# A two-layer graph kernel: the second scatter of the edges' sums is split 73 to 25 between two layers in place of 49 to 49

## The chip, the cores and the metric

The kernel runs on one core of a Trainium2 chip. A core has a matrix engine (TensorE, "PE" in the profile, with its weight loads as "PEld"), a vector engine (VectorE, "DVE"), a scalar engine (ScalarE, "ACT"), GpSimd ("POOL") and a sync engine ("SP") that here only issues transfers. 16 DMA engines carry out all transfers. The metric is the device time of one execution in microseconds (us), lower is better. A profiled execution gives a trace beside its time.

## The reference

A graph network over 50,000 nodes with 256 features each and 12,500 edges, sorted by destination. Only what touches the stages below is shown:

```python
edge_feat = gelu((x[src] + edge_attr) @ W_pre + b_pre) * bases     # 12500 x 256
aggr = segment_sum(edge_feat, dst, num_segments=50000)
y = x + aggr
h = relu(bn(y @ W1 + b1, g1, be1))        # bn: mean and variance over all 50,000 nodes
h = relu(bn(h @ W2 + b2, g2, be2))
x = layernorm(x + (y + h))                # = layernorm(2*x + aggr + h)
# then a second, relational layer on 10,000-odd rows reached by edges, and a last layernorm
```

The first layernorm needs 2x + aggr + h. The kernel keeps one array `y` in device memory. First it holds x + aggr, which the two layers read. For the last step it has to hold x + aggr/2, because the third stage multiplies it by two. So aggr is scattered into `y` twice: first whole, and later once more with the factor -1/2.

## The kernel before, in words

One program per engine; the order of the work is written out by hand and engines wait for each other by semaphores. The nodes are cut into 98 blocks of 512 rows, the edges into 98 tiles of 128 edges. The stages, with their times in the profiled execution:

- **Edges** (to about 255 us): messages per edge, their sums per destination in the array `sums` in on-chip memory; x is copied to `y`.
- **Layer 1** (blocks g = 0 to 97, about 230 to 622 us): SyncE loads block g of `y` into a ring of four buffers (line 713), PE turns it (eight transposes, line 767), ACT and DVE split it into two parts (lines 795 and 848), PE multiplies each block in 24 wide matmuls over three precisions (lines 58 to 60), DVE takes the batch statistics of the product (line 564, two instructions per block), ACT copies the product out of PSUM into one of four `d_h` buffers (`out`, line 817) and SyncE stores it to `scratch_h` (line 719). ACT's copy of a block waits until the store of four blocks earlier has landed. The last four blocks stay on chip (`d_held`) and are not stored.
- **Between the layers**: DVE joins the statistics (lines 594 to 606). One step of it is done by POOL, `coef_pool` (line 610, a power of -1/2). Nothing of layer 2 can start before it.
- **Layer 2** (g = 98 to 195, about 626 to 953 us): the same products with other weights. A block comes from `scratch_h`, passes ReLU with the batch-norm coefficients (line 803), and its product goes to `scratch_h` again.
- **Third stage** (`dense3`, to about 1385 us) and the relational layer (`edges1`, to the end).

POOL carries out both scatters. A tile of 128 sums is one indirect DMA with addition into rows of `y` (`scatter_tile`, line 616). The first scatter runs from 206 us into layer 1. Then comes the second one, `take_back(t)` for t = 0 to 97. Each call waits on three things: that ACT has multiplied the tile's piece of `sums` by -1/2 (`halve`, line 822), that PE has turned every block of `y` into which the tile's rows fall (`passed`), and that the scatter four tiles earlier has landed. Between two of them POOL has to run `coef_pool`. A number, `early`, says how many of the 98 tiles stand ahead of it. POOL runs its instructions in order, so all tiles ahead of `coef_pool` are issued first. The third stage may not read `y` before all 98 have landed.

Of the kernel before, what the change touches and what calls it, by code (L numbers as in the profile page):

```python
# [644 lines left out]
def dense12(nc, A, K, S, c, used, block, first):  # L645
# [9 lines left out]
        return used[-1]  # L655

    NB, ET = S.NB, S.ET
    early = ET // 2
    passes = [(1, k) for k in range(NB)] + [(2, (NB - HELD + n) % NB) for n in range(NB)]
    loads = [g for g, (layer, k) in enumerate(passes) if layer == 1 or k < NB - HELD]  # L660
    stores = [g for g, (layer, k) in enumerate(passes) if layer == 2 or k < NB - HELD]
# [962 lines left out]
def build(nc, A, nodes, edges):  # L1624
# [9 lines left out]
    with ExitStack() as c:  # L1634
# [11 lines left out]
        with ExitStack() as inner:  # L1646
# [33 lines left out]
            block = inner.enter_context(nc.Block())  # L1680
            first = edges0(nc, A, K, S, inner, used, block)
            second = dense12(nc, A, K, S, inner, used, block, first)
            dense3(nc, A, K, S, inner, used, block, second)
        edges1(nc, A, K, S)
# [64 lines left out]
```

How the kernel before makes its waits and increments, by code:

```python
def wait(engine, semaphore, value):  # L72
    if not (isinstance(value, int) and value <= 0):
        engine.wait_ge(semaphore, value)
# [114 lines left out]
    @block.sync  # L190
# [1 line left out]
        def load_attr(k):  # L192
            if k >= 4:
                sp.wait_ge(lo_done, k - 3)
            sp.dma_start(attr[:, k % 4], A["attr_t"][k]).then_inc(attr_full[k % 4], 16)
# [1 line left out]
        def load_bases(k):  # L197
            if k >= 3:
                sp.wait_ge(msg_done, k - 2)
            sp.dma_start(bases[:, k % 3], A["bases_t"][k]).then_inc(bases_full[k % 3], 16)
        sp.dma_start(K.src[:], A["src_t"]).then_inc(src_full, 16)
        sp.dma_start(run_i[:], A["dst_r"]).then_inc(run_full, 16)
        sp.dma_start(before_i[:], A["before_r"]).then_inc(run_full, 16)
        load_attr(0)
        sp.dma_start(raw_w0, A["w0"]).then_inc(w0_full, 16)
        sp.dma_start(K.cols[:], A["cols"]).then_inc(cols_full, 16)
        load_attr(1)
        load_bases(0)
        sp.wait_ge(run_done, 1)
        sp.dma_start(A["cont"].rearrange("(t p) -> t p", p=P), run[:]).then_inc(run_kept, 16)
        sp.dma_start(dst_i[:], A["dst_t"]).then_inc(index_full, 16)
        sp.dma_start(nxt_i[:], A["next_t"]).then_inc(index_full, 16)
# [1 line left out]
        sp.dma_start(last_i[:], A["tile_last"]).then_inc(index_full, 16)  # L215
        sp.dma_start(rel_i[:], A["rel_r"]).then_inc(rel_i_full, 16)
        sp.wait_ge(run_kept, 16)
        sp.dma_start(cont[:], A["cont"].rearrange("(a e) -> a e", a=1).to_broadcast([P, S.TC * P])).then_inc(cont_full, 16)
```

## Time and profile before

| | |
|---|---|
| median of 3 runs | 2051.4 us (2044.15 to 2055.25) |
| profiled execution, its own time | 2051.5 us |
| its span | 2049.7 us |
| granted TensorE clock, mean over the span | 0.957 |
| layer 1: last block's statistics | 621.7 us |
| layer 2: first and last block's statistics | 635.3 and 952.0 us |
| second scatter: tiles 0 to 48, last issued at | 561.2 us |
| second scatter: tiles 49 to 97, issued | 626.3 to 728.2 us |

The page of the profile gives the busy share of each engine over the whole span, but the kernel is a sequence of stages with different limits. So the numbers of use here are those of a stretch: how often a block comes out, what the engines wait for in that stretch, and how long a transfer takes from its issue to its landing. A block's statistics (line 564) are a good clock: two instructions per block, and those that read `pU` and those that read `pS` belong to alternate blocks.

### The profile page before, as it was taken

The numbers are of one execution on the slowest core, as the hardware profiler recorded it, in microseconds if no ns is written. First come the engines' busy times: TensorE is split into PE (matmuls) and PEld (weight loads), VectorE is DVE, ScalarE is ACT, GpSimd is POOL, SyncE is SP. The second block draws the span as 40 slices with busy tenths as digits, with TensorE's granted clock in tenths as the row PEclk, the third lists the DMA queues.
The fourth block names the chain that finished last, engine by engine and source line by source line (L and its number), as shares of the span: only waits on it lengthen the run. The fifth ranks groups of instructions, "written<-read, shape, count | busy, mean of one in ns | idle before, by whom it ended". The sixth has DMA issues, their size and how long they took to land. (4 is left out here: it accounts for less than half of the span.)

```text
span 2049.7 us, 27458 instructions
## 1 busy us (share of the span) xinstructions
PE 1797.7 (88%) x8697; PEld 1401.3 (68%) x8697; DVE 1604.4 (78%) x2326; ACT 1298.1 (63%) x1818; POOL 1074.7 (52%) x1200
## 2 busy tenths in 40 slices
PE   4577589999998889998999999955999999999994
PEld 3465468888886566675666666634887888888883
DVE  4688456767667889996999999984787888888883
ACT  2334346666656788886788888862665666666663
POOL 7456546767706820000555656557787764444443
PEclk9899799999999999999999999987999999999997
DMA  9999999999997999998999999965555422222210
GB/s 351 360 356 396 356 358 337 337 343 330 339 303 199 340 360 325 337 321 318 351 386 386 388 388 383 392 254 161 160 159 170 124 80 69 69 71 74 65 42 28
DMA packets 194033, 541.42 MB, mean 264 GB/s; under 512 B 27013, under 2 KB 77295, under 8 KB 193506
## 3 DMA queue, kind: packets, MB, share of 16 engines
q1 hardware_dynamic: 136354, 414.86, 55.4%
q0 software_dynamic: 47136, 73.62, 15.6%
q10 hardware_dynamic: 10400, 51.20, 6.5%
q8 instruction: 70, 1.15, 0.2%
q14 instruction: 73, 0.60, 0.1%
HBM read 341.49 MB, written 253.66 MB: 290 GB/s over the span
## 5 line engine op out<-in xcount | busy, mean ns | idle before, releaser
L616 POOL DMA_INDIRECT scratch_y<-sums,k_target x196 | 315.2, 1608 | 159.8 <-issue 72.4
L1005 ACT ACTIVATE d_o<-d_u,d_free 128x256 f32<-128x256 f32 x392 | 203.2, 589 | 66.3 <-POOL d_free L1042 66.3
L978 PE MATMUL d_pN<-d_y,d_free 128*128 128x512 f32 x392 | 193.3, 616 | 43.0 <-DVE d_u L1068 34.0
L983 PEld LDWEIGHTS d_pN<-k_ident,d_r 128*128 128x128 f32 x1568 | 191.5, 193 | 47.3 <-issue 46.8
L58 PE MATMUL pU<-d_part_h,k_w_h 128*128 128x512 f32 x392 | 166.3, 424 | 38.5 <-DVE d_part_l L860 17.1
L983 PE MATMUL d_pN<-k_ident,d_r 128*128 128x128 f32 x1568 | 191.6, 276 | 0.0
L848 DVE TENSOR_TENSOR d_part_l<-pT,d_part_h 128x1024 fp32r<-128x1024 f32 x98 | 119.9, 1224 | 86.0 <-ACT d_part_h L795 86.0
L795 ACT ACTIVATE d_part_h<-pT 128x1024 fp32r<-128x1024 f32 x98 | 100.5, 1026 | 132.1 <-PE pT L767 118.4
L58 PE MATMUL pS<-d_part_h,k_w_h 128*128 128x512 f32 x392 | 165.5, 422 | 15.3 <-ACT d_h L817 9.2
L1039 POOL TENSOR_TENSOR d_free<-d_free,k_minus_half 128x8 f32<-128x8 f32 (+1 forms) x100 | 163.7, 1637 | 0.2
L1068 DVE SCALAR_TENSOR_TENSOR d_u<-d_pN,d_free,k_base 128x256 f32<-128x256 f32 x392 | 161.1, 474 | 0.0
L254 POOL DMA_INDIRECT k_ring<-in_x,k_src x100 | 121.9, 1219 | 68.3 <-PE pT L282 39.8
L994 ACT ACTIVATE d_r<-d_h,k_coef 128x512 f32<-128x512 f32 x196 | 147.7, 800 | 15.5 <-DMA d_h<-scratch_h 15.5
L59 PE MATMUL pU<-d_part_l,k_w_h 128*128 128x512 f32 x392 | 156.6, 400 | 0.0
L60 PE MATMUL pU<-d_part_h,k_w_l 128*128 128x512 f32 x392 | 156.3, 399 | 0.0
L60 PE MATMUL pS<-d_part_h,k_w_l 128*128 128x512 f32 x392 | 156.0, 398 | 0.0
L59 PE MATMUL pS<-d_part_l,k_w_h 128*128 128x512 f32 x392 | 155.8, 398 | 0.0
L610 POOL TENSOR_TENSOR d_bn_rstd<-d_bn_var,k_minus_half 128x2 f32<-128x2 f32 x2 | 1.5, 730 | 281.1 <-DVE d_bn_var L597 281.1
L1433 ACT ACTIVATE e_gate<-pG,k_gate_b 128x512 f32<-128x512 f32 (+1 forms) x150 | 98.3, 672 | 76.8 <-PE pG L60 76.7
L803 ACT ACTIVATE d_r<-k_ring,d_coef 128x512 f32<-128x512 f32 x188 | 141.7, 803 | 0.0
L978 PEld LDWEIGHTS d_pN<-d_y,d_free 128*128 128x128 f32 x392 | 67.1, 191 | 106.0 <-issue 105.4
L1241 POOL DMA_INDIRECT e_xd<-out,k_dst_gather x98 | 124.6, 1272 | 26.7 <-issue 26.7
(219 smaller groups left out, 4946.3 us busy)
## 6 DMA issues: line engine op xcount, KB each, us to landing
scratch_h<-d_h SPq DMA_DIRECT2D x192, 512.0 KB, 7.7
out<-d_o SPq DMA_DIRECT2D x97, 520.0 KB, 5.9
k_ring<-scratch_y SPq DMA_DIRECT2D x98, 512.0 KB, 7.7
d_h<-scratch_h SPq DMA_DIRECT2D x98, 512.0 KB, 7.0
d_y<-scratch_y SPq DMA_DIRECT2D x98, 512.0 KB, 7.8
scratch_y<-in_x ACTq DMA_DIRECT2D x25, 2000.0 KB, 19.7
k_ring<-scratch_h SPq DMA_DIRECT2D x94, 512.0 KB, 5.6
attr<-in_attr_t SPq DMA_DIRECT2D x25, 512.0 KB, 15.2
```

The source lines that it names most:

```text
L58: pe.matmul(out, lhs[0], rhs[0], start=first, stop=False)
L59: pe.matmul(out, lhs[0], rhs[1], start=False, stop=False)
L60: return pe.matmul(out, lhs[1], rhs[0], start=False, stop=last)
L616: pool.indirect_dma_start(out=A["y"], out_offset=bass.IndirectOffsetOnAxis(ap=K.target[:, t:t + 1], axis=0), in_=K.sums[:, t], in_offset=N ...
L803: last = act.activation(r[:, g % 2, cc], source(g)[:, cc * B:(cc + 1) * B], ACT.Relu, bias=coef[:, 1, cc:cc + 1], scale=coef[:, 0, cc:cc + 1])
L978: pe.matmul(pN[k % 4][:, 2 * two:2 * two + 2].rearrange("p j f -> p (j f)"), twice[:], y[:, k % 4, two * 2 * F:(two + 1) * 2 * F], start=T ...
L983: last = pe.matmul(pN[k % 4][:, j, cc * P:(cc + 1) * P], r[:, k % 4, cc, j * P:(j + 1) * P], K.ident[:], start=False, stop=j % 2 == 1 and ...
L994: last = act.activation(r[:, k % 4, cc], h2[:, k % 4, cc * B:(cc + 1) * B], ACT.Relu, bias=K.coef2[:, 1, cc:cc + 1], scale=K.coef2[:, 0, c ...
L1005: last = act.activation(o[:, k % 4, j, 0:F], u[:, k % 3, j], ACT.Identity, bias=nb[:, n, j:j + 1], scale=rs[:, n, J + j:J + j + 1])
L1039: pool.tensor_tensor(out=rs[:, at, now], in0=v[:, at, now], in1=K.minus_half[:, now], op=ALU.pow).then_inc(rs_done, 1)
L1068: last = dve.scalar_tensor_tensor(out=u[:, k % 3, j], in0=pN[k % 4][:, j], scalar=rs[:, (k - 3) % 4, j:j + 1], in1=K.base[:], op0=ALU.mult ...
L1241: pool.indirect_dma_start(out=xd[:, k % 2, j], out_offset=None, in_=A["out"], in_offset=bass.IndirectOffsetOnAxis(ap=K.dst_gather[:, t:t + ...
```

## The change

One number: of the 98 tiles, three quarters (3 * 98 // 4 = 73) are scattered ahead of `coef_pool` instead of half (49). 24 tiles move from behind the layers' boundary to the end of layer 1.

```diff
     NB, ET = S.NB, S.ET
-    early = ET // 2
+    early = 3 * ET // 4
...
         for t in range(early):
             take_back(t)
         coef_pool(pool)
         for t in range(early, ET):
             take_back(t)
```

Only POOL's program moves; the rows on the other engines stay as they are. First place: POOL behind tile 48, before. L616 is the scatter of a tile, L736 the reading of its `passed` value, L610 the power of `coef_pool`.

```order
L736 TENSOR_LOAD k_passed
L736 ISA x2
L616 DMA scratch_y<-sums,k_target 50000x256
L610 TENSOR_TENSOR d_bn_rstd<-d_bn_var,k_minus_half 128x2
L736 TENSOR_LOAD k_passed
```

The same place of the changed kernel:

```order
L736 TENSOR_LOAD k_passed
L736 ISA x2
L616 DMA scratch_y<-sums,k_target 50000x256
L736 TENSOR_LOAD k_passed
L736 ISA x2
L616 DMA scratch_y<-sums,k_target 50000x256
```

The power no longer follows tile 48; the tiles go on. Second place: POOL behind tile 72 of the changed kernel, 24 tiles later.

```order
L736 TENSOR_LOAD k_passed
L736 ISA x2
L616 DMA scratch_y<-sums,k_target 50000x256
L610 TENSOR_TENSOR d_bn_rstd<-d_bn_var,k_minus_half 128x2
L736 TENSOR_LOAD k_passed
L736 ISA x2
```

Here the power stands now, with 25 tiles behind it instead of 49.

## Rows read from the trace of the kernel before

**Rows 1.** The page: the whole span, and PE and DMA in 40 slices.

```profile
span 2049.7 us, 27458 instructions
PE 1797.7 (88%) x8697; PEld 1401.3 (68%) x8697; DVE 1604.4 (78%) x2326; ACT 1298.1 (63%) x1818; POOL 1074.7 (52%) x1200
...
PE   4577589999998889998999999955999999999994
...
DMA  9999999999997999998999999965555422222210
```

**Rows 2.** Windows of both layers: busy us of each engine (instructions), clock, DMA share, GB/s.

```profile
440.00:550.00 110.00, 110.00 (x600) 92.32 (x599) 76.78 (x99) 68.00 (x70) 76.60 (x51) 1.00 1.09 336
550.00:574.00 24.00, 23.60 (x124) 18.99 (x123) 16.01 (x19) 14.05 (x14) 10.20 (x7) 1.00 1.07 346
574.00:620.00 46.00, 46.00 (x250) 38.58 (x249) 31.67 (x39) 23.32 (x24) 0.00 (x0) 1.00 0.93 288
620.00:635.00 15.00, 6.72 (x20) 5.00 (x19) 7.24 (x14) 7.45 (x9) 8.22 (x6) 0.66 0.27 30
680.00:740.00 60.00, 49.18 (x195) 35.31 (x196) 46.59 (x60) 46.20 (x57) 40.96 (x26) 1.00 1.09 346
740.00:950.00 210.00, 200.49 (x796) 144.16 (x795) 194.66 (x253) 180.29 (x219) 0.00 (x0) 1.00 0.96 328
```

**Rows 3.** Line 564, every second block, six stretches: duration, first and last start.

```profile
L564 DVE BATCH_NORM_STATS2 stats<-pU x68: 680/690/702, 301.3 to 544.4; 128x6 f32<-128x512 f32 x68
...
L564 DVE BATCH_NORM_STATS2 stats<-pU x7: 682/699/700, 551.3 to 574.8; 128x6 f32<-128x512 f32 x7
...
L564 DVE BATCH_NORM_STATS2 stats<-pU x14: 680/692/700, 574.8 to 619.5; 128x6 f32<-128x512 f32 x14
...
L564 DVE BATCH_NORM_STATS2 d_stats<-pU x16: 681/687/699, 635.3 to 680.4; 128x6 f32<-128x512 f32 x16
...
L564 DVE BATCH_NORM_STATS2 d_stats<-pU x18: 680/687/700, 679.8 to 739.9; 128x6 f32<-128x512 f32 x18
...
L564 DVE BATCH_NORM_STATS2 d_stats<-pU x30: 680/688/700, 771.9 to 860.1; 128x6 f32<-128x512 f32 x30
```

**Rows 4.** POOL's scatters (line 616) in three stretches, the same columns.

```profile
L616 POOL DMA_INDIRECT scratch_y<-sums,k_target x7: 1541/1541/1542, 549.4 to 561.2; - x7
...
L616 POOL DMA_INDIRECT scratch_y<-sums,k_target x26: 1535/1636/2513, 626.3 to 680.4; - x26
...
L616 POOL DMA_INDIRECT scratch_y<-sums,k_target x23: 1541/1543/2294, 682.2 to 728.2; - x23
```

**Rows 5.** ACT's waits in 550 to 574, then in 680 to 740: total us, times, longest.

```profile
ACT d_h L817 <- DMA scratch_h<-d_h: 8.8, 6, 1.9
...
ACT d_h L817 <- DMA scratch_h<-d_h: 14.6, 14, 1.5
```

**Rows 6.** Stores, median us to landing: 540-560, 580-600, 640-660, 700-720.

```profile
scratch_h<-d_h SPq DMA_DIRECT2D x5, 512.0 KB, 12.5
...
scratch_h<-d_h SPq DMA_DIRECT2D x6, 512.0 KB, 5.1
...
scratch_h<-d_h SPq DMA_DIRECT2D x6, 512.0 KB, 9.0
...
scratch_h<-d_h SPq DMA_DIRECT2D x6, 512.0 KB, 12.3
```

**Rows 7.** What the added tiles wait for: ACT's halving (all), PE's transposes up to 562 us.

```profile
L822 ACT ACTIVATE sums<-sums x25: 1046/1062/1062, 292.8 to 559.8; 128x1024 f32<-128x1024 f32 x25
...
L767 PE MATMUL pT<-k_ident,k_ring x664: 270/273/418, 230.9 to 559.8; 128*128 128x128 f32 x166
```

**Rows 8.** POOL in order of time: start us, us, [idle before <- what ended it].

```profile
625.01 0.73 POOL L610 TENSOR_TENSOR d_bn_rstd<-d_bn_var,k_minus_half 128x2 f32<-128x2 f32 x1 [62.24 <-DVE d_bn_var L597]
...
736.22 0.56 POOL L1019 TENSOR_SCALAR d_free<-k_ident 128x128 f32<-128x128 f32 x1 [6.00 <-DMA scratch_y<-sums,k_target]
```

**Rows 9.** DMA queues in 440 to 560 us: packets, MB, share of 16 engines.

```profile
q1 hardware_dynamic: 9301, 33.87, 74.1%
q0 software_dynamic: 7890, 6.37, 34.3%
...
scratch_y<-sums,k_target POOLq DMA_INDIRECT x56, 7.8
```

## Prediction, made before the changed kernel was run

> **What bounds the kernel now.** I began with the page [rows 1]. PE is busy 88% of the span, DMA stands at 9 tenths from the start to slice 25 or so, and neither says what a moved scatter is worth, since the layers at issue cover only 230 to 953 us. So I read windows inside the layers [rows 2]. At 440 to 550 us PE is busy for all 110 us while DMA's share is already at 1.09: PE sets the pace, DMA is full beside it. At 680 to 740 us, with scatters running in layer 2, PE is busy only 49 of 60 us and DMA again at 1.09: there DMA sets the pace. Once the scatters are over (740 to 950) PE is at 200 of 210 and DMA at 0.96.
>
> The third view is the clock of blocks [rows 3]. The rows hold two instructions for every second block, and "last" is the second of its pair, 0.6 us after the first. This gives us per block:
> - layer 1 with scatters, 301.3 to 543.8: 66 blocks, 3.67.
> - 551.3 to 574.8: 6 blocks, 3.92.
> - layer 1 without scatters, 574.8 to 618.9: 12 blocks, 3.67.
> - layer 2 with scatters, first part, 635.3 to 679.8: 14 blocks, 3.18.
> - second part, 679.8 to 739.3: 16 blocks, 3.72.
> - layer 2 without scatters, 771.9 to 859.4 or so: 28 blocks, 3.125.
>
> So the scatters cost nothing for a long time and then something. The waits name the place [rows 5]: in both slow stretches ACT's copy of the product (line 817) waits for the store of four blocks earlier. The landing times say why it comes late [rows 6]: a store lands in 5.1 us without scatters, 9.0 us shortly after they begin in layer 2, 12.3 and 12.5 us in the slow stretches. DMA falls behind a little with each block, the backlog grows for about 50 us of layer 2 until four buffers no longer cover it, and only then do blocks slow down. That is the idea on which everything below rests.
>
> **The change part by part.** 24 tiles (49 to 72) are issued from 563 us on instead of behind `coef_pool`. Nothing is added or removed; each costs POOL the same and moves the same bytes.
>
> *Can they be issued there?* Three waits. Halving: the last of 25 pieces is multiplied at 559.8 us [rows 7], so all are ready. The transposes: destinations are sorted and spread evenly, so tile t of 98 needs about t + 2 blocks turned; tile 72 needs about 74. By 562 us 664 transposes of 8 per block are done, 83 blocks [rows 7]. The third wait is the scatter four tiles back, and sets the rate: 7 scatters from 549.4 to 561.2, 1.97 us each [rows 4]. So 24 more end at 561.2 + 24 x 1.97 = 608.5 us. POOL is wanted again for the power at 625.0 and idles 62.24 us before it [rows 8]; 16 us of that would be left. `coef_pool` is not late. It would be, if a scatter took over 2.66 us (63.8/24), as none in a group of rows does on average: 26 of them take 54.1 us in layer 2, 2.16 each.
>
> *Layer 1's end.* The stretch 574.8 to 618.9 now runs beside scatters, with DMA's backlog already at its limit: ACT waits for stores in 550 to 574. The steady price there is the pace after the backlog has bitten: about 4.0 us a block (3.92 on average over 6 blocks, of which the first and last are at the turn), 0.33 over the 3.67 of PE. The blocks that can be hit are those between 563 and the last scatter's end, about 12. Three of them are slow already in the kernel before, since the backlog takes that long to go (blocks until 574.8). That leaves 9 blocks x 0.33 = 3.0 us lost. The bounds: 0, if the slow blocks at 550 to 574 were a passing thing, since for the 66 blocks before them scatters at the same rate cost nothing; and 12 x 0.6 = 7 us, if blocks here slow by as much as those of layer 2 did (3.72 - 3.12). I take 3.0, from the nearest rows.
>
> *The boundary.* The last stores of layer 1 are those of the blocks before the held four. DMA's share between 620 and 635 us is 0.27 [rows 2], and the last moved tile should have landed by about 617 (608.5 + 7.8, the median to landing [rows 9]). The backlog has time to empty, so layer 2 starts as it does now. Price 0.
>
> *Layer 2.* What the scatters cost here before: 14 blocks x (3.18 - 3.125) = 0.8 us, 16 blocks x (3.72 - 3.125) = 9.5 us, together 10.3. Now 25 tiles stand behind the power instead of 49. The first 26 of before are issued from 626.3 to 680.4 [rows 4], so the last of the 25 goes out at about 678.5. This is where the expensive part begins. The 0.8 us stays. The backlog that has built up has to go: in both places of before the slow pace outlasts the last scatter by about three blocks, which at 0.5 each is 1.5 us. So 2.3 us stay and 8.0 go. The bounds: 9.5 gone (no tail), and half of 10.3, 5.1 (if the price per scatter were even). I take 8.0. What is late next when the store wait goes is PE's own pace at 3.125.
>
> *Behind layer 2.* The third stage may read `y` from 953 on; the scatters were through at 736 [rows 8] and will be through near 687. Nothing waits for them either way: 0. From there on everything moves forward by what the two layers gained.
>
> The sum: 2051.5 (the profiled execution's own time, which is the 2049.7 of the span and 1.8 around it) + 3.0 - 8.0 = 2046.5 us. The median of the runs shown is 2051.4, so I take the sum for the median too. A difference under 0.5%, 10.3 us, can't be told from no change by a measurement of this kernel, whose three runs are 11.1 us apart. The forecast is 0.24% down.
>
> *A page weighed against the rows.* Between 440 and 560 us the 56 scatters occupy 34.3% of the 16 engines and the rest 74.1% [rows 9], together over 100: the two kinds of traffic do compete. The Trainium skill (DMA: Bandwidth & Descriptors, "Issuing engines are not separate DMA queues") says that transfers issued by sync, scalar and GpSimd end up on the same 16 DMA engines and interleave. By this rule alone the change would be worth nothing, because the same work waits in the same queue at another time; that is rival B. The trace agrees that the engines are shared, and shows that the price is not even: 66 blocks of layer 1 paid nothing.
>
> **The rivals.**
> - *A: layer 1 takes the tiles free.* For it: 3.67 us a block over 66 blocks with scatters; 550 to 574 may be the crest of a wave. Against it: the landing time had climbed to 12.5 us when the slow blocks came, and scatters that go on leave it no reason to fall. Time: 2051.5 - 8.0 = 2043.5; with no tail in layer 2 as well, 2042.
> - *B: the price moves with the tile.* 24 of 49 tiles take half of 10.3 = 5.1 us with them and cost the same in layer 1. For it: DMA is at 1.07 to 1.09 in both places. Against it: PE needs 3.67 us a block in layer 1 and 3.125 in layer 2, so layer 1 leaves DMA 0.55 us a block more. Time: 2051.5.
> - *C, the slower side: the backlog is carried over the boundary.* If the moved tiles' traffic is not through when layer 2's first stores and loads go out, at about 637 us, layer 2 starts with buffers already late and pays from its first block: 14 blocks x 0.6 = 8.3 us and the tail of 1.5, so 9.8 of the 10.3 stay, while layer 1 has lost 3 to 7. Time: 2051.5 - 0.5 + 3 to 7 = 2054 to 2058. It decides only if scatters take over 2.66 us each; then `coef_pool` is late too. Against it: DMA's 0.27 in 620 to 635 and the 16 us left on POOL.
> - *D: the tiles do not move in time*, because tile 49 to 72 wait for their blocks. By [rows 7] nothing of it is to be seen: they go out at once. It would be 2051.5 with a late power.
>
> **How the numbers follow.** Forecast 0.55, A 0.20, B 0.14, C 0.09, D 0.02. The forecast's own bounds are 3.0 lost (0 to 7) and 8.0 gained (5.1 to 9.5): 2042 to 2053.4. The median of a few runs adds some us either way. A range of 2040 to 2054.5 holds the forecast, A, B and the lower end of C. Faster by over 0.5% means below 2041.1: A with runs that fall low, and a small part of the forecast, 0.13. Slower by over 0.5%, above 2061.7: C beyond what I worked out, 0.04. Within 0.5%: 0.83.
>
> **What would show it.** In the changed kernel's profile:
> - POOL: 24 more scatters from 563 to about 609 us, then some 16 us idle before line 610, which starts near 628.
> - Line 564 at 575 to 611 us: 4.0 us a block instead of 3.67; ACT's line 817 waits for `scratch_h` stores there, which land in 12 us.
> - Layer 1's last statistics at about 624.7 instead of 621.7.
> - Layer 2: blocks at 3.18 for the first 14, two or three slow ones, then 3.125; the store wait of 14.6 us [rows 5] shrinks to 2 or so.
> - Layer 2 ends about 5 us earlier than 952.
>
> I am wrong if the blocks at 575 to 611 stay at 3.67 (A), if line 610 starts after 632 or the first blocks of layer 2 already wait for stores (C), or if layer 2 shows 3.4 us a block for all the time that scatters run (B).

## The result, and the profile after

The changed kernel takes 2042.87 us (median of 16 runs), the kernel before 2048.82 us (16 runs). The ratio is 0.9963, with a 95% interval of 0.995 to 0.9976: 5 to 10 us faster. The forecast was 5.0 us faster. The profiled executions are further apart, 2049.7 against 2042.5 us of span, and only part of those 7.2 us belongs to the change. The single times of one kernel spread over more than the difference (2042.12 to 2057.48 and 2036.13 to 2046.78 us), so what the change did is read from the stages of the traces.

POOL first: the moved tiles in layer 1 (with the tile before them), then the tiles of layer 2 (line 616 of the kernel after; count, min/median/max ns, first and last start, as in [rows 4]):

```profile
L616 POOL DMA_INDIRECT scratch_y<-sums,k_target x25: 1541/1541/1543, 561.0 to 610.1; - x25
...
L616 POOL DMA_INDIRECT scratch_y<-sums,k_target x25: 1535/1632/2441, 627.7 to 679.8; - x25
```

The 24 moved tiles went out from 563 to 610.1 us, 2.05 us apart (24 intervals in the 49.1 us from 561.0), and 25 were left for layer 2. POOL at the boundary, as in [rows 8]:

```profile
626.43 0.73 POOL L610 TENSOR_TENSOR d_bn_rstd<-d_bn_var,k_minus_half 128x2 f32<-128x2 f32 x1 [14.74 <-DVE d_bn_var L597]
```

POOL still waits 14.74 us for DVE before the power of `coef_pool`. So nothing at the boundary is late because of the moved tiles. The scatters are through at about 688 instead of 736 us.

Windows of the kernel after, for three of the stretches of [rows 2]:

```profile
574.00:620.00 46.00, 45.73 (x244) 37.52 (x243) 30.43 (x37) 25.43 (x25) 28.34 (x19) 1.00 1.09 343
620.00:635.00 15.00, 6.73 (x23) 5.01 (x22) 8.35 (x15) 7.45 (x9) 7.12 (x5) 0.71 0.35 82
680.00:740.00 60.00, 55.54 (x222) 39.85 (x221) 52.98 (x68) 50.84 (x62) 3.26 (x2) 1.00 1.01 346
```

Two lines changed most. At 574 to 620 DMA is now at 1.09 instead of 0.93, yet PE still gets through 45.73 of 46 us. At 680 to 740 PE is busy 55.5 us instead of 49.2. ACT's waits for stores in 574 to 620 and in 680 to 740 (before: none and 14.6 [rows 5]):

```profile
ACT d_h L817 <- DMA scratch_h<-d_h: 15.2, 11, 1.7
...
ACT d_h L817 <- DMA scratch_h<-d_h: 4.0, 3, 1.5
```

The 15.2 us of waiting in 574 to 620 cost the blocks only about 1.5 us; why is said at the end of the experiments. For the length of layer 2 I take line 564 over the whole of it. The first block reads `pU`, the last reads `pS`, so the length runs from the first start of the one row to the last start of the other. Before, then after:

```profile
L564 DVE BATCH_NORM_STATS2 d_stats<-pU x98: 680/687/700, 635.3 to 949.6; 128x6 f32<-128x512 f32 x98
L564 DVE BATCH_NORM_STATS2 d_stats<-pS x98: 497/682/700, 638.6 to 952.6; 128x6 f32<-128x512 f32 x96, 128x6 f32<-128x336 f32 x2
```

```profile
L564 DVE BATCH_NORM_STATS2 d_stats<-pU x98: 680/686/700, 636.9 to 944.4; 128x6 f32<-128x512 f32 x98
L564 DVE BATCH_NORM_STATS2 d_stats<-pS x98: 496/682/700, 640.0 to 947.4; 128x6 f32<-128x512 f32 x96, 128x6 f32<-128x336 f32 x2
```

That is 952.6 - 635.3 = 317.3 us before and 310.5 us after: layer 2 is 6.8 us shorter. The end of layer 2 comes 5.2 us earlier (947.4 against 952.6), because layer 1 had begun 1.6 us later in this execution. The other 2.0 us of the span's 7.2 arise in the relational layer, behind everything that was changed.

### The profile page after: what moved, and what is told of

Same layout as the page of the kernel before. It is cut to its first block and busy times, and to the rows that moved or that the text cites. A ratio compares the mean times of both kernels' runs of the same rounds, so it can differ in the third digit from the quotient of the medians.

```text
span 2042.5 us, 27458 instructions
## 1 busy us (share of the span) xinstructions
PE 1795.9 (88%) x8697; PEld 1398.3 (68%) x8697; DVE 1604.1 (79%) x2326; ACT 1297.4 (64%) x1818; POOL 1067.5 (52%) x1200
## 3 DMA queue, kind: packets, MB, share of 16 engines
q1 hardware_dynamic: 136354, 414.86, 55.5%
## 5 line engine op out<-in xcount | busy, mean ns | idle before, releaser
L616 POOL DMA_INDIRECT scratch_y<-sums,k_target x196 | 312.0, 1592 | 159.7 <-issue 71.4
L610 POOL TENSOR_TENSOR d_bn_rstd<-d_bn_var,k_minus_half 128x2 f32<-128x2 f32 x2 | 1.5, 729 | 275.9 <-DVE d_bn_var L597 275.9
```

The source lines that it names most:

```text
L616: pool.indirect_dma_start(out=A["y"], out_offset=bass.IndirectOffsetOnAxis(ap=K.target[:, t:t + 1], axis=0), in_=K.sums[:, t], in_offset=N ...
```

## The experiments

All differ from the kernel before by the lines shown (e5 from the changed kernel). "Paced" means that POOL holds each tile back until a certain number of blocks is done. Two lengths are read from each trace, both from the starts of the statistics: layer 2 as above, and the last 40 block intervals of layer 1, less the 146.05 us that they take when nothing waits for a store (146.06 in six of the traces). This difference is the price in layer 1. The ratio isn't the quotient of the two medians, and differs from it by up to 0.0024.

| kernel | tiles in layers 1 / 2 | layer 1 price, us | layer 2, us | median | before, run beside it | ratio (95%) |
|---|---|---|---|---|---|---|
| before | 49 / 49 | 1.6 | 317.3 | 2048.82 | | |
| after | 73 / 25 | 1.5 | 310.5 | 2042.87 | 2048.82 | 0.9963 (0.9950 to 0.9976) |
| e1 | 49 / none | 0.0 | 306.6 | 2039.76 | 2052.61 | 0.9952 (0.9934 to 0.9970) |
| e2 | 49 / 25 | 0.0 | 310.7 | 2044.66 | 2052.61 | 0.9965 (0.9948 to 0.9982) |
| e3 | 24 / 74 | 0.0 | 323.6 | 2057.77 | 2052.61 | 1.0035 (1.0020 to 1.0050) |
| e4 | 80 / 18 | 0.0 | 307.5 | 2046.78 | 2052.61 | 0.9974 (0.9958 to 0.9990) |
| e5 | 73 / 25 paced | 2.6 | 308.1 | 2044.36 | 2053.11 | 0.9945 (0.9923 to 0.9967) |
| e6 | 49 / 49 paced | 0.0 | 307.1 | 2042.71 | 2053.11 | 0.9946 (0.9932 to 0.9959) |
| e7 | 49 / 49, 3 buffers | 3.5 | 327.2 | 2068.08 | 2053.11 | 1.0064 (1.0047 to 1.0081) |
| e8 | 98 / none | 1.7 | 306.5 | 2078.96 | 2053.11 | 1.0125 (1.0108 to 1.0143) |
| e9 | 49 / 49 | 1.4 | 318.7 | 2084.57 | 2085.13 | 0.9997 (0.9969 to 1.0024) |
| e10 | 73 / 25 | 1.5 | 310.1 | 2084.57 | 2085.13 | 0.9988 (0.9953 to 1.0023) |
| e11 | 44 / 54, both paced | 0.0 | 309.5 | 2074.38 | 2085.13 | 0.9972 (0.9943 to 1.0002) |
| e12 | 49 / 49 paced | 0.6 | 307.2 | 2074.85 | 2085.13 | 0.9954 (0.9918 to 0.9990) |

### e1: no tiles in layer 2

```diff
-        for t in range(early, ET):
+        for t in range(early, LEFT):        # LEFT = 49, and the waits at the end for as many
             take_back(t)
```

> Left out of the computation: tiles 49 to 97 of the second scatter, all those of layer 2; layer 1 keeps its 49. Backlog theory (scatters cost nothing until DMA has fallen four stores behind, then about 0.6 us a block): layer 2 runs at 3.125 us a block from its first block on, 10.3 us less than before, ratio 0.995; layer 1 as before with its slow blocks near 550 to 574. Even price theory (every tile costs about 0.21 us wherever it runs beside layer 2): the same 10.3 us. This run sets the size of the whole price; both fall if it gains under 5 us.

```profile
L565 DVE BATCH_NORM_STATS2 d_stats<-pU x98: 679/686/700, 630.4 to 934.0; 128x6 f32<-128x512 f32 x98
L565 DVE BATCH_NORM_STATS2 d_stats<-pS x98: 496/682/701, 633.5 to 937.0; 128x6 f32<-128x512 f32 x96, 128x6 f32<-128x336 f32 x2
```

937.0 - 630.4 = 306.6 us (line 565 here, one line lower). The whole price of the 49 tiles in layer 2 is 10.7 us, 10.3 expected. But the slow blocks of layer 1 near 550 to 574 are gone too, and nothing was changed there. That was the first sign that they come and go by themselves. e1 and e2 leave out scatters that the result needs, so only their times are of use.

### e2: 49 in layer 1, 25 in layer 2, 24 left out

The edit is that of e1 with LEFT = 74.

> Left out: tiles 74 to 97 of the second scatter; 49 tiles run in layer 1 and 25 in layer 2, so it differs from the changed kernel by 24 tiles fewer in layer 1 and from the kernel before by 24 fewer in layer 2. Backlog theory: the 25 tiles of layer 2 cost 2.3 to 3.6 us in all, so 6.7 to 8.0 us less than before. Even price: 24 x 0.21 = 5.1 us less than before, the 25 left cost 5.2. If the 24 moved tiles cost something in layer 1, this kernel is faster than the changed one by that: 3.0 us as I forecast it, 0 if layer 1 takes them free.

Layer 2 lasts 310.7 us, as in the changed kernel. So 25 tiles cost 4.1 us and the last 24 cost 6.6 us, where an even price would be 5.5 and 5.2. This favours the backlog theory, but not as clearly as I had forecast (2.3 to 3.6 us stay). The blocks are slow here from 664 us on. The median is no lower than that of the changed kernel, measured each against its own "before": 24 tiles fewer in layer 1 bring nothing that the medians show, though its trace has no slow block there.

### e3 and e4: 24 and 80 tiles ahead of the power

```diff
-    early = ET // 2
+    early = ET // 4        # e3; 80 in e4
```

> The change turned round: 24 tiles ahead of the power, 74 behind it. Backlog theory: the 25 added tiles all fall into the slow part, 50 us at 3.72 us a block, 13.4 blocks x 0.6 = 8 us more in layer 2, and layer 1 loses its slow blocks at 550 to 574 (1.6 us less): 6.4 us slower than before, ratio 1.003. Even price: 25 x 0.21 = 5.2 us slower. Layer 1 is at 3.67 us a block to its end in both. The number of slow blocks in layer 2 tells: 29 or so behind the first 14, by the backlog theory at the same 3.72.

> 80 tiles ahead of the power, 18 behind it. POOL: the 14.7 us of idle time ahead of the power in the changed kernel hold 7 tiles at 2.0 us, so the power comes at the same time, within 1 us. Backlog theory: 18 tiles run out at about 665 us, before four buffers are used up, so layer 2 has no slow block and loses under 1.5 us instead of 3.6: 2 us faster than the changed kernel, if layer 1 takes 7 more tiles at no price; about 8 us faster than before. Even price: 7 x 0.21 = 1.5 us faster than the changed kernel with every block of layer 2 a little slower while scatters run.

Layer 2 of e4 lasts from 632.4 to 939.9 us. Now the price in layer 2 can be set against the number of tiles that start at its beginning, over e1's 306.6: 0 tiles 0, 18 tiles 0.9, 25 tiles 3.9 to 4.1, 49 tiles 10.7 (12.1 in e9), 74 tiles 17.0 us, of which 1.5 are another thing (a block interval of 4.8 us at 873 us, see e5). The first 18 cost 0.05 us each, those behind them 0.26 on average (14.6 us for 56). So there is a threshold, and an even price is out. e3 is 5.2 us slower than before by medians, 6.4 expected; its 25 added tiles cost 6.3 us where I had 8, and 4.8 without those 1.5, so behind the threshold the price per tile is smaller than I had taken it. e4 is faster than before (5.8 us by medians, 8 expected), but not to be told from the changed kernel (0.9974 and 0.9963, each against other runs of before). It saves 3.0 us of layer 2 by its trace; the expected 2 us over the changed kernel is neither shown nor refuted by the times.

### e5 and e6: the same tiles, further apart

```diff
+            if t > early:
+                pool.wait_ge(h_done, NB + 2 * (t - early))      # e5, with early = 73
+                pool.wait_ge(h_done, NB + 1 * (t - early))      # e6, with early = 49
             scatter_tile(pool, A, K, t, halved_in, bound)
```

> The changed kernel, with its 25 tiles of layer 2 held back to one for every two blocks (each waits until 2 x its number blocks of layer 2 are copied out). Backlog theory: the same 25 tiles, but DMA keeps up, stores land in 6 to 7 us throughout, and layer 2 costs what it costs without scatters: 305.9 to 306.9 us from its first to its last statistics, against 309.9 in the changed kernel; 3 to 4 us faster than the changed kernel, 9 to 10 faster than before. Even price: 25 tiles still cost 4 us, 309.9 us.

> The kernel before, with its 49 tiles of layer 2 held back to one per block (3.1 us instead of 2.12 us apart). Backlog theory: DMA falls behind by 0 to 0.2 us a block instead of 0.5, so over 49 blocks the four buffers nearly cover it: layer 2 lasts 306 to 309 us against 316.7 before, 8 to 10 us faster than before, as much as the change or more, with no tile moved to layer 1. Even price: 316.7 and no gain.

Layer 2 of e6, and then the landing of its stores at 660 to 680 and 700 to 720 us:

```profile
L564 DVE BATCH_NORM_STATS2 d_stats<-pU x98: 678/685/701, 636.5 to 940.6; 128x6 f32<-128x512 f32 x98
L564 DVE BATCH_NORM_STATS2 d_stats<-pS x98: 497/681/699, 639.6 to 943.6; 128x6 f32<-128x512 f32 x96, 128x6 f32<-128x336 f32 x2
...
scratch_h<-d_h SPq DMA_DIRECT2D x7, 512.0 KB, 7.5
...
scratch_h<-d_h SPq DMA_DIRECT2D x7, 512.0 KB, 8.6
```

This decides it. The same 49 tiles in the same layer, with the same bytes, cost 0.5 us instead of 10.7 when they come one per block. Stores land in 7.5 and 8.6 us where they took 10.8 at 660 to 680 and 12.3 at 700 to 720 [rows 6]. What was paid for is not the traffic but its rate. e6 leaves all tiles where they were and gains 10.4 us by medians, ratio 0.9946; the change gained 6.0. e5, with fewer tiles in layer 2, is no faster (0.9945): there is little left to move, and its trace paid 2.6 us in layer 1, where e6 paid nothing.

The 1.5 us by which layer 2 of e5 is longer than that of e1 are not the scatters' either. They are one block interval of 4.6 us that ends at 869 us, long after the last tile (790 us). PE's first instruction of that block and the window behind it (granted clock 0.50, DMA 0.64), and then the same place in the kernel before:

```profile
864.18 0.80 PE L58 MATMUL pU<-d_part_h,k_w_h 128*128 128x512 f32 x1 [2.22 <-DVE d_part_l L862]
864.00:867.30 3.30, 3.12 (x7) 2.48 (x8) 2.56 (x4) 3.27 (x5) 0.00 (x0) 0.50 0.64 159
...
871.00 0.50 PE L58 MATMUL pU<-d_part_h,k_w_h 128*128 128x512 f32 x1 [2.22 <-DVE d_part_l L860]
```

In both PE has been idle for 2.22 us, because DVE is late: in front of block 70 it has joined a part of the batch statistics (line 580). In e5 the clock is then granted at half, 1.2 instead of 2.4 GHz, in the whole of this window, and a wide matmul takes 0.63 us instead of 0.40. In the kernel before it stays at 1.00. The same interval, block 72 of layer 2, is long in five of the fourteen traces (e3, e5, e7, e10 and e11; 4.6 to 4.8 us instead of 3.2), with the clock down in each. What decides between the two isn't shown.

### e7: three store buffers

```diff
-    full, stored = K.ring_full, [sem(f"stored{n}") for n in range(4)]
+    full, stored = K.ring_full, [sem(f"stored{n}") for n in range(NH)]      # NH = 3
...
-            if g in store_no and store_no[g] >= 4:
-                act.wait_ge(stored[store_no[g] % 4], 16 * (store_no[g] // 4))
+            if g in store_no and store_no[g] >= NH:
+                act.wait_ge(stored[store_no[g] % NH], 16 * (store_no[g] // NH))
```

> The kernel before with three d_h buffers in use instead of four (the memory of the fourth stays unused). ACT's copy then waits for the store of three blocks earlier; the store may take about 8 us from issue to landing instead of 12. Backlog theory: the slow blocks of layer 2 begin near 645 us instead of 680, and its price rises from 10.7 to about 15 us; layer 1, where stores land in 7 to 11 us beside scatters, gets slow blocks from about 480 us on, 3 to 8 us more. 8 to 12 us slower than before. If the loads' ring and not the store buffers were the limit, nothing changes.

Stores of e7 at 660 to 680 and 700 to 720 us:

```profile
scratch_h<-d_h SPq DMA_DIRECT2D x5, 512.0 KB, 8.2
...
scratch_h<-d_h SPq DMA_DIRECT2D x6, 512.0 KB, 7.9
```

Blocks are slow as soon as stores take 8 us instead of 12, as forecast: the number of `d_h` buffers sets how much backlog is free. The slow blocks of layer 2 begin 23 us behind its first block (667.2 against 644.2) where it was 48 us before (683.8 against 635.3). The price is above what I expected, 20.6 us in layer 2 (15) and 15 by medians (8 to 12). Part of it falls between 878 and 893 us, far behind the scatters, in two intervals of 7.2 and 4.6 us. The first is 1.9 us longer than in the other traces, and ACT waited 2.1 us for a store just before it, so three buffers are scarce even without scatters. The second is the drop of the clock described under e5.

One rival needs no run: that POOL's scatters slow DVE down. In layer 2 the statistics on DVE take 687 ns in the slow stretch and 688 in the free one [rows 3].

### e8: all tiles ahead of the power

The edit is `early = ET`.

> All 98 tiles ahead of the power. POOL needs until about 658 to 661 us for them (49 more at 1.85 to 2.0 us from 563 on), so line 610 comes near 660 instead of 625: 35 us lost at the boundary, and layer 2 free of scatters gives 10.7 back: 24 us slower than before, ratio 1.012. The point from which the boundary pays, by POOL's idle time of 14.7 us in the changed kernel, is tile 80. If tiles could be issued faster than 1.85 us each, less is lost.

```profile
654.66 1.30 POOL L610 TENSOR_TENSOR d_bn_rstd<-d_bn_var,k_minus_half 128x2 f32<-128x2 f32 x1
```

The power starts at 654.7, and layer 2's first statistics at 665.0 instead of 635.3. Layer 2 has its free length of 306.5. By medians it is 25.9 us slower (24 expected). This is the cliff that the 14.74 us of POOL's idle time stood for.

### e9 to e12: second traces, and pacing on both sides

e9 and e10 are the kernel before and the changed one, e12 is e6, each unchanged. e11 paces both sides:

```diff
+            if t != early:                                      # early = 44
+                pool.wait_ge(h_done, NB + t - early if t > early else 52 + t)
             scatter_tile(pool, A, K, t, halved_in, bound)
```

> The kernel before, unchanged, for a second trace. Open is the price in layer 1: its last 40 blocks took 1.6 us over PE's pace in the first traces of both kernels, 2.6 with 73 tiles and paced layer 2, and nothing with 80. If that price is set by chance from one execution to the next and not by the number of tiles, it comes out elsewhere between 0 and 2.6 us here, while layer 2 stays at 316 to 318 us. If it belongs to the kernel, it is 1.6 again.

> The changed kernel, unchanged, for a second trace. By chance: the price in layer 1 is between 0 and 2.6 us, not 1.5 again; my own forecast of 3.0 more than before would show 4 or more. Layer 2 lasts 309.5 to 310.5 us in either case, and line 610 starts 14 to 15 us after POOL's last tile.

> 44 tiles ahead of the power and 54 behind it, both paced to one per block. DMA has at most one tile beside a block everywhere, so by the backlog theory layer 1 ends with no slow block in any execution (146.1 us from block 57 to 97) and layer 2 lasts 306 to 307 us: as fast as 49 paced or 0 to 2 us faster, 9 to 11 us faster than before, 3 to 5 faster than the changed kernel. If pacing did not matter in layer 1, slow blocks of 3.8 to 4.0 us still appear there after 540 us.

> 49 tiles in layer 2 paced to one per block, for a second trace and a comparison on one chip with the others of this call. Backlog theory: layer 2 lasts 306 to 307 us again, against 309.9 of the changed kernel; faster than the changed kernel by 3.5 us, less the chance in layer 1.

These ran on another chip, and there all kernels take some 30 us more. The `pX` transposes of the relational layer (line 1309) run from 1396.2 to 1979.7 us in the kernel before and from 1398.0 to 2015.5 us in e9. The stage begins 1.8 us later and ends 35.8 us later, so the extra time lies in a stage that no experiment touches. It also scatters the times (2067 to 2090 us for e10 alone), and by medians nothing of the change is left here: the interval of e10's ratio, 0.9953 to 1.0023, takes in 1. The layers themselves repeat better. Layer 2: 318.7 us before and 310.1 after, a gain of 8.6, and of 10.1 without the drop of the clock that e10 has and e9 hasn't; e12 307.2. Layer 1: 1.4 us before, 1.5 after, 0.6 for e12. POOL is idle for 11.1 us ahead of the power in e10, where 14 to 15 were expected. By its median e12 is 10.3 us faster than before, its ratio 0.9954 is again below 1 with its whole interval.

e11 is a miss in part. Layer 1 has no slow block, as expected, but layer 2 lasts 309.5 us where I had 306 to 307. About 1.4 us of it comes in small delays between 720 and 800 us, with the last of its 54 tiles, and about 1.5 is the drop of the clock, in an interval of 4.8 us that ends at 861. It is no faster than 49 paced.

### Why waits in layer 1 cost so little

ACT's waits for stores from 510 to 620 us (total, times, longest) in the kernel before, the changed one and e4. Their prices in layer 1 are 1.6, 1.5 and 0.0 us:

```profile
ACT d_h L817 <- DMA scratch_h<-d_h: 18.3, 16, 1.9
...
ACT d_h L817 <- DMA scratch_h<-d_h: 18.6, 16, 1.7
...
ACT d_h L817 <- DMA scratch_h<-d_h: 11.3, 16, 1.1
```

e4's blocks wait just as often as those of the others, and its stores land in 11.8 us at 580 to 600 (12.2 in the changed kernel), yet no block of it is slow. The reason is in ACT's own rows. Where nothing waits for stores, ACT is idle all the same in each block, until PE's transposes are done (before):

```profile
575.68 1.03 ACT L795 ACTIVATE d_part_h<-pT 128x1024 fp32r<-128x1024 f32 x1 [1.72 <-PE pT L767]
```

A wait for a store uses up this idle time first. Block by block over blocks 67 to 93 of all traces, single waits under 0.8 us delayed nothing, while those of 1.6 to 1.8 us delayed the next blocks by 0.3 us on average. In layer 2 ACT has less room: it is idle for 0.44 us a block in 740 to 950, against 1.81 us in 574 to 620 in layer 1 ([rows 2]: 29.7 us over 67.2 blocks and 22.7 us over 12.5). There 14.6 us of waits went with 9.5 us of lost time.

## Why the prediction was right, and which terms were off

The forecast of 2046.5 stood 5.0 us below the profiled execution of before, and the medians moved by 6.0. The mechanism is the one given: DMA falls behind while scatters are issued back to back, the store buffers cover it for a time, and then blocks slow down. e3 and e4 show the threshold, e6 shows that the rate and not the amount costs, and e7 that the number of buffers sets the threshold. Two terms were off in the first pair of traces, and their errors of 3.1 and 1.2 us have opposite signs. That the sum came out so near is in part luck.

- **Issue at the end of layer 1:** right. 608.5 us forecast for the last moved tile, 610.1 measured; 16 us of idle time forecast, 14.7 measured.
- **Layer 1's end, 3.0 us lost:** wrong, and this is the larger error. The price is 1.6 us before and 1.5 after, and 1.4 and 1.5 in the second pair, so the change added nothing that either pair shows. ACT waits for stores and the stores land in 12 us, as forecast. But the forecast turned every such wait into a block slower by 0.33 us, and left out that ACT is idle for 1.7 us a block there anyway: in the changed kernel the ten blocks from 571 to 609 us took 3.82 us on average, not 4.0. I had also read six slow blocks in one trace as the steady state of that stretch. Six of the twelve other traces have no slow block there (e1 to e4, e6 and e11), e4 with 80 tiles among them, and e5 with 73 tiles paid 2.6. What makes the difference from one execution to the next isn't shown. With 49 tiles or fewer the price is 0 to 1.6 us, 0.5 on average over eight traces (e7 left out, with its other buffers), and with 73 or more 0 to 2.6, 1.5 on average over five. A cost of about 1 us for the moved tiles is thus possible.
- **The boundary, 0:** right. DMA's share between 620 and 635 us rose only to 0.35, and layer 2's first 14 blocks took 3.19 us each ((681.5 - 636.9)/14), where it was 3.18 before.
- **Layer 2, 8.0 us gained:** 6.8 measured, 8.6 in the second pair. My 2.3 us that stay were 3.9 and 3.5, the latter 2.0 without the drop of the clock. In the first trace the tail was dearer than three blocks at 0.5: two blocks of 4.2 and 4.3 us among the five after 681.5. The 10.3 us that the scatters cost before were 10.7 and 12.1.
- **Behind layer 2, 0:** the scatters were through before 688 us, as forecast. The 2.0 us by which the span gained there is of the size by which that stage varies: from the last statistics to the end of the span it took 1097.1 us before and 1095.1 after, and 1096 to 1099 in e1 to e8.

Rival A, that layer 1 takes the tiles free, was nearer for that one term. Its 2043.5 is also nearer to the median than the forecast, but only because the median of before came out 2.6 us lower with 16 runs than with 3; by the difference A is 2.0 us off and the forecast 1.0. Rival B (the price moves with the tile) fell with e6, and the Trainium skill's rule beside it, that all issuing engines share the 16 DMA engines (DMA: Bandwidth & Descriptors, "Issuing engines are not separate DMA queues"), agrees with the trace of before (both kinds of traffic together took 108.4% of the 16 engines' time in 440 to 560 us [rows 9]) but doesn't give the price: here the shared engines cost time only where the backlog outlasted the buffers and ACT's idle time. Rival C's mechanism at the boundary was not seen; POOL being late was shown with e8, at 98 tiles and not at 73.

The version to prefer is e6: the tiles stay split 49 to 49, and those of layer 2 go out one per block. It beats the kernel before in both comparisons. Against the changed kernel the intervals of the ratios overlap; by the traces layer 2 is shorter by 3.4 us in the first and by 2.9 in the second (1.4 without the drop of the clock), and the price in layer 1 is lower by 1.5 and 0.9.

## What to carry to other kernels

Before moving background transfers to another stage, spread them out where they are. Traffic that a stage can absorb at one piece per block may cost half a microsecond, and back to back twenty times that. A stall that begins some 50 us after its cause can be a backlog outgrowing a ring of buffers: follow the time from issue to landing through the stage, not only the share of busy time. Before a wait is priced, look at how long the waiting engine is idle without it: 15 us of waits cost 1.5 us in a layer where ACT had 1.7 us to spare in every block. And take slow blocks of a single trace near a limit for a chance until a second trace has them too.

## What the runs showed of the hardware

- The same block intervals are long in every trace, whatever the scatters do: those of blocks 34 and 66 of layer 1 (5.0 and 5.3 us instead of 3.67) and of blocks 38 and 70 of layer 2 (at least 5.0 and 5.3 instead of 3.12), 32 blocks apart within a layer. The program sets them: in front of each stand the two aggregates of line 580 on DVE, 1.9 us together (before: at 388.9, 506.5, 764.3 and 865.6 us), which join 32 blocks of the statistics. In layer 1 the blocks behind make up for it (2.35 us behind block 34, 2.33 and 3.39 behind block 66). In layer 2 the two places cost about 1.3 and 2.2 us in the free run of e1, which is no part of the scatters' price.
- PE idled 2.22 us at block 72 of layer 2 in all fourteen traces. In five of them the granted clock then fell to 1.2 GHz for a part of the block, which cost 1.3 to 1.6 us; in nine it stayed at 2.4 GHz.
- In e9 to e12, all on one chip, the relational layer took 610 to 630 us from the first `pX` transpose to the last, and 582 to 586 in the other ten traces. Layer 2 of the kernel before took 317.3 and 318.7 us. Whether the chip or the time sets this isn't shown.
- A scatter took POOL 1.54 us beside layer 1 in every case in the changed kernel (561.0 to 610.1) and 1.54 to 2.44 us beside layer 2.
